# Attention edge pass: keys and values added in one instruction, one value in four added by GpSimd, one mask in four made by VectorE, and another order of the work on VectorE and ScalarE

## The chip, the cores and the metric

The kernel runs on one core of a Trainium2 chip. The time is the device time of one execution in microseconds (us), and a kernel is judged by the median of several runs. The core has five engines that run beside each other and meet only at semaphores: TensorE (PE in the rows; PEld is its weight load), VectorE (DVE), ScalarE (ACT), GpSimd (POOL) and SyncE (SP), which here only starts transfers.

## What is computed

A graph network on 6250 nodes of 256 numbers and 100000 edges, sorted by their destination. First a weighted sum over the edges with two linear layers and a normalization, then two transformer convolutions with 4 heads of 64 channels, then a last normalization. Nearly all the time that matters here goes to the two convolutions:

```
e = (edge_attr @ We).reshape(-1, H, C)
kj = k[src] + e
vj = v[src] + e
logits = jnp.einsum('ehc,ehc->eh', q[dst], kj) / np.sqrt(C)
m = jax.lax.stop_gradient(jax.ops.segment_max(logits, dst, num_segments=n))
ex = jnp.exp(logits - m[dst])
denom = jax.ops.segment_sum(ex, dst, num_segments=n)
a = ex / (denom[dst] + 1e-16)
agg = jax.ops.segment_sum(vj * a[:, :, None], dst, num_segments=n)
return agg.reshape(n, H * C) + x @ Ws + bs
```

## The kernel before

`edge_pass_attention` runs twice, as phases e1 and e2, one for each convolution. A step `i` handles one tile of 128 edges, one edge per partition, and there are T = 832 steps in a pass. Steps are counted in batches of 26 (`BATCH`, 32 batches a pass), after each of which a softmax over the batch's logits is worked off in eight small stages, two steps apart (`PACE`); and in quads of four (`QUAD`, 208 a pass), because some work is done once for four steps. Each engine has its own program, a loop over the steps, and takes its instructions strictly in that order.

What one step does, engine by engine:

- GpSimd gathers the key and value rows of the 128 source nodes from HBM into `kv`, a ring of NG = 6 tiles (line 1303, a DMA whose descriptors GpSimd makes itself). Gather `i` waits until VectorE has read the tile of step `i - 6` (`vj_done`). Once in a quad it also makes `pick` for four steps (line 1294), the one-hot matrix with which TensorE later fetches the queries.
- TensorE multiplies the edge attributes by `We` into PSUM (`e_e` in the rows, lines 1315 and 1316; each matmul stands as two instructions in the trace). In every fourth step of a quad this product isn't computed: it was made in an earlier phase, and SyncE loads it into `made`. Then TensorE fetches the queries (line 1325), and, 43 steps later, sums the weighed values by node with the matrix `mask` (line 1366).
- VectorE adds the edge's product to the keys (line 1416) and to the values (line 1420) in two instructions of 256 columns, takes four dot products of 64 columns, one for each head (line 1428), and adds an earlier step's sums to the accumulator `acc` (line 1510). The stages of the softmax stand behind that.
- ScalarE works 42 steps (LAG) behind: it makes the one-hot `mask` of step `n = i - LAG` by two activations of 128x128 (lines 1561 and 1567) and weighs the values by four activations of 65 columns, one for each head (line 1571). Its share of the softmax (lines 1543, 1546, 1551 and 1554) stands ahead of that in a step. For the last 42 steps of a pass (`LATE`), VectorE makes the mask and weighs the fourth head.

The keys and the values lie in `kvj`: two tiles for keys, and a ring of NV = 44 for values. The softmax's exponent on ScalarE (line 1546) waits for a subtraction on VectorE (line 1474). The loops for VectorE and ScalarE in the kernel before:

```
for i in range(END):
    if i < T:
        logits(i)
    if LATE <= i - LAG < T:
        late_part(i - LAG)
    if 0 <= i - LAG - 2 < T:
        add_sums(i - LAG - 2)
...
    j, step = step_at(i)
    if j is not None:
        softmax(j, step)
```

## Time and profile before

| | us |
|---|---|
| median of 3 runs | 4820.88 (4820.83 to 4821.61) |
| the profiled execution, its own time | 4832.06 |
| its span | 4830.3 |
| e1, first to last gather on GpSimd | 1365.2 to 2908.6 |
| e2, first to last gather on GpSimd | 3126.3 to 4640.0 |
| busy over the span: PE, DVE, ACT, POOL | 87%, 83%, 62%, 65% |

The profile is of one execution. Its shares are means over phases of very different kinds; the two attention passes are the two stretches in which ScalarE is busy. Durations of neighbouring instructions on VectorE, ScalarE and TensorE overlap a little in the trace, because one starts while the one before drains: what one costs its engine is the distance from start to start.

### The profile page before, as it was taken

How to read it: one execution, taken by the hardware profiler on the slowest of the kernel's cores; microseconds unless marked ns; L12 is line 12 of the kernel's file. 1: busy time of each engine (PE TensorE's matmuls, PEld its weight loads, DVE VectorE, ACT ScalarE, POOL GpSimd, SP SyncE). 2: the span in 40 equal slices, each digit the busy share in tenths (PEclk: the TensorE clock that was granted, in tenths of full speed). 3: DMA queues.
4: the chain of work that ended last, by engine and by line, in shares of the span. 5: the costliest groups of instructions: out<-in, count | busy, mean ns of one | idle time of the engine just before them, and what ended most of it. 6: DMA issues, size and time to landing. Idle time of an engine off the chain costs nothing. (4 is left out here: it accounts for less than half of the span.)

```text
span 4830.3 us, 107746 instructions
## 1 busy us (share of the span) xinstructions
PE 4189.2 (87%) x17694; PEld 3210.6 (66%) x17694; DVE 3989.0 (83%) x22772; ACT 2982.2 (62%) x10607; POOL 3116.4 (65%) x2996
## 2 busy tenths in 40 slices
PE   2887887888979999999999998889999999999988
PEld 2766666675547777777777774567777777777755
DVE  4655555556869999999999998789999999999986
ACT  1111111112319898989898984149999999989971
POOL 6677777740067777777777771287777777777730
PEclk9999999999999999999999999999999999999989
DMA  4666666654568887878788773587777777777734
GB/s 121 189 192 196 192 193 193 191 167 149 169 212 237 233 236 232 233 229 236 231 234 228 231 230 104 173 247 231 226 230 228 231 228 227 226 228 231 226 114 149
DMA packets 663064, 996.73 MB, mean 206 GB/s; under 512 B 99667, under 2 KB 489690, under 8 KB 662407
## 3 DMA queue, kind: packets, MB, share of 16 engines
q0 software_dynamic: 171408, 540.40, 38.1%
q1 hardware_dynamic: 491000, 449.44, 30.8%
q14 instruction: 471, 3.86, 0.3%
q8 instruction: 185, 3.03, 0.3%
HBM read 870.01 MB, written 119.44 MB: 205 GB/s over the span
## 5 line engine op out<-in xcount | busy, mean ns | idle before, releaser
L1303 POOL DMA_INDIRECT e_kv<-kv,src x1664 | 1635.0, 983 | 748.1 <-DVE e_kvj L1420 449.7
L1571 ACT ACTIVATE e_vals<-e_kvj,e_ex 128x65 f32<-128x65 f32 x6572 | 1725.1, 334 | 5.5 <-PE e_sum L1366 5.1
L1366 PE MATMUL e_sum<-e_vals,e_mask 128*128 128x260 f32 x3328 | 1063.7, 403 | 206.2 <-ACT e_vals L1571 190.0
L1325 PE MATMUL e_q<-q,e_pick 128*128 x3328 | 1017.2, 387 | 95.3 <-DVE e_logit L1428 66.4
L1428 DVE CUSTOM_DVE_ANT_0 e_kvj<-e_kvj,e_q 128x64 f32<-128x64 f32 x6656 | 1060.2, 214 | 3.4 <-PE e_q L1325 2.2
L152 POOL DMA_INDIRECT e_x<-x_rows,e_src x783 | 747.3, 954 | 263.1 <-issue 172.3
L1366 PEld LDWEIGHTS e_sum<-e_vals,e_mask 128*128 128x128 f32 x3328 | 563.0, 190 | 454.4 <-issue 379.7
L1325 PEld LDWEIGHTS e_q<-q,e_pick 128*128 128x128 f32 x3328 | 618.2, 191 | 252.4 <-issue 169.9
L1315 PE MATMUL e_e<-e_we,e_ea 112*128 112x256 f32 x2496 | 752.3, 382 | 17.4 <-DMA e_ea<-attr_tiles 16.2
L1316 PE MATMUL e_e<-e_we,e_ea 112*128 112x256 f32 x2496 | 745.8, 380 | 0.0
L1510 DVE TENSOR_TENSOR acc<-acc,e_sum 128x260 f32 x1664 | 697.3, 419 | 41.4 <-issue 23.6
L530 ACT ACTIVATE q<-e_edges 128x512 f32<-128x512 f32 x208 | 124.2, 597 | 925.5 <-PE e_edges L523 921.7
L1294 POOL TENSOR_SCALAR e_pick<-e_spots,own 128x512 f32<-128x512 bf16 x416 | 660.9, 1589 | 15.4 <-DMA e_spots<-locals 1.1
L1567 ACT ACTIVATE e_mask<-e_apart,one 128x128 f32<-128x128 f32 x1580 | 634.6, 402 | 52.5
L597 PE MATMUL e_sum<-e_x,e_mask 128*128 x1664 | 455.2, 400 | 210.6 <-DVE e_mask L612 114.0
L620 DVE TENSOR_TENSOR acc<-acc,e_sum 128x256 f32 x832 | 349.9, 421 | 332.0 <-PE e_sum L597 308.0
L1561 ACT ACTIVATE e_apart<-iota,local 128x128 f32<-128x128 f32 x1580 | 610.4, 386 | 0.0
L1416 DVE TENSOR_TENSOR e_kvj<-e_kv,e_e 128x256 f32<-128x256 f32 x1248 | 513.4, 411 | 66.2 <-DMA e_kv<-kv,src 40.3
L1315 PEld LDWEIGHTS e_e<-e_we,e_ea 112*128 112x128 f32 x2496 | 477.7, 192 | 96.4 <-issue 20.3
L1420 DVE TENSOR_TENSOR e_kvj<-e_kv,e_e 128x256 f32<-128x256 f32 x1248 | 514.7, 412 | 21.0 <-ACT e_vals L1571 20.6
L1428 DVE DVE_READ_ACCUMULATOR2_ANT e_logit<- 128x1 f32 x6656 | 531.6, 80 | 0.2 <-issue 0.2
L597 PEld LDWEIGHTS e_sum<-e_x,e_mask 128*128 128x128 f32 x1664 | 316.9, 198 | 312.2 <-issue 270.2
(223 smaller groups left out, 4479.1 us busy)
## 6 DMA issues: line engine op xcount, KB each, us to landing
e_ea<-attr_tiles SPq DMA_DIRECT2D x1248, 112.0 KB
edges<-q SPq DMA_DIRECT2D x208, 256.0 KB
e_spots<-locals SPq DMA_DIRECT2D x416, 128.0 KB
e_made<-edges SPq DMA_DIRECT2D x416, 128.0 KB
e_kv<-kv,src POOLq DMA_INDIRECT x1664
kv<-n_proj_rows SPq DMA_DIRECT2D x98, 256.0 KB
q<-attr_tiles SPq DMA_DIRECT2D x208, 112.0 KB
n_x<-x_rows SPq DMA_DIRECT2D x98, 128.0 KB
```

The costliest lines, as they stand in the source:

```text
L152: e.indirect_dma_start(out=self.x[:, at:at + D], out_offset=None, **rows_of(self.t["x_rows"], self.src[:, i:i + 1])).then_inc(self.got[i / ...
L597: e.matmul(sums[i % SUMS][:, 0:D], mask[:, i % R, :], rows, start=True, stop=True).then_inc(summed, 1)
L1294: e.tensor_scalar(pick[:, c % 2, :], spots[:, c % 2, :], k["own"][:, 0:1], None, ALU.is_equal).then_inc(picked, 1)
L1303: e.indirect_dma_start(out=kv[:, u, :], out_offset=None, **rows_of(kv_rows, k["src"][:, i:i + 1])).then_inc(kv_got[u], 16)
L1315: e.matmul(pe_e[a % 2][:, 0:D], ea[:, a % NE, 0:P], we[:, 0, :], start=True, stop=False)
L1316: e.matmul(pe_e[a % 2][:, 0:D], ea[:, a % NE, P:2 * P], we[:, 1, :], start=False, stop=True).then_inc(e_done, 1)
L1325: e.matmul(pe_q[i % 2][:, 0:D], pick[:, c, at:at + P], rows, start=True, stop=True).then_inc(q_done, 1)
L1366: e.matmul(sums[n % 2][:, 0:VALS], mask[:, n % R, :], vals[:, n % R, :], start=True, stop=True).then_inc(summed, 1)
L1428: dot = e.tensor_tensor_reduce(kvj[:, i % 2, h, 0:C], kvj[:, i % 2, h, 0:C], pe_q[i % 2][:, hs], 1.0, 0.0, ALU.mult, ALU.add, logit[:, j % ...
L1510: e.tensor_tensor(rows, rows, sums[n % 2][:, 0:VALS], ALU.add).then_inc(added, 1)
L1567: e.activation(mask[:, n % R, :], apart[:], ACT.Relu, bias=k["one"][:, 0:1], scale=-1.0).then_inc(masked, 1)
L1571: by_weight = e.activation(vals[:, n % R, h * HV:(h + 1) * HV], kvj[:, 2 + n % NV, h, :], ACT.Copy, scale=ex[:, b % 2, h, r:r + 1])
```

## The change

Three things change inside `edge_pass_attention`, and nothing outside it.

In three steps of four the two additions become one instruction of 512 columns that reads the edge product twice. In the fourth step of each quad VectorE adds only the keys, and GpSimd adds the values (`last_values`), between two gathers; the next gather waits for that addition, since it overwrites the tile that the addition reads, and the load of `made` waits for it too.

The mask of every fourth step, those with `n % QUAD == 0`, is made by VectorE in one comparison (`make_mask`), where ScalarE took two activations. In the late steps VectorE makes all masks, as before, now by this function.

The order changes. On VectorE, the dot products of a step move from behind its additions to behind the mask, the late part and the addition to `acc`. On ScalarE, the mask and the weighing move ahead of the softmax's part.

The core of the diff:

```diff
+        def vector_masks(n):
+            return n >= LATE or n % QUAD == 0
+
+        def vector_masks_before(n):
+            return -(-min(n, LATE) // QUAD) + max(n - LATE, 0)
+
...
                 def load_made(c):
                     if c >= 2:
-                        e.wait_ge(vj_done, (c - 1) * QUAD)
+                        e.wait_ge(kvj_done, (c - 1) * QUAD)
+                        e.wait_ge(values_done, c - 1)
...
+                def last_values(c):
+
+                    i = QUAD * c + QUAD - 1
+                    e.wait_ge(kv_got[i % NG], 16 * (i // NG + 1))
+                    e.wait_ge(made_got[c % 2], 16 * (c // 2 + 1))
+                    if i >= NV:
+                        e.wait_ge(weighed, i - NV + 1)
+                    by_head = "p (h c) -> p h c"
+                    e.tensor_tensor(kvj[:, 2 + i % NV, :, 0:C], kv[:, i % NG, D:].rearrange(by_head, h=H),
+                                    made[:, c % 2, :].rearrange(by_head, h=H), ALU.add).then_inc(values_done, 1)
+
+                def gather(i):
+                    u = i % NG
+                    if i >= NG:
+                        e.wait_ge(kvj_done, i - NG + 1)
+                        if (i - NG) % QUAD == QUAD - 1:
+                            last_values((i - NG) // QUAD)
+                            e.wait_ge(values_done, (i - NG) // QUAD + 1)
+                    e.indirect_dma_start(out=kv[:, u, :], out_offset=None,
+                                         **rows_of(kv_rows, k["src"][:, i:i + 1])).then_inc(kv_got[u], 16)
+
                 e.memset(kvj[:], 1.0).then_inc(ones_set, 1)
+                e.wait_ge(ones_set, 1)
                 for i in range(T):
-                    u = i % NG
                     if i % QUAD == 2:
                         pick_rows(i // QUAD)
-                    if i >= NG:
-                        e.wait_ge(vj_done, i - NG + 1)
-                    e.indirect_dma_start(out=kv[:, u, :], out_offset=None,
-                                         **rows_of(kv_rows, k["src"][:, i:i + 1])).then_inc(kv_got[u], 16)
-                e.wait_ge(ones_set, 1)
+                    gather(i)
+                for c in range((T - NG) // QUAD, s.quads):
+                    last_values(c)
 
...
                     if i >= 2:
                         e.wait_ge(dots_done, i - 1)
-                    e.tensor_tensor(kvj[:, i % 2, :, 0:C], kv[:, i % NG, 0:D].rearrange("p (h c) -> p h c", h=H), edge,
-                                    ALU.add).then_inc(kj_done, 1)
-                    if i >= NV:
-                        e.wait_ge(weighed, i - NV + 1)
-                    e.tensor_tensor(kvj[:, 2 + i % NV, :, 0:C], kv[:, i % NG, D:].rearrange("p (h c) -> p h c", h=H), edge,
-                                    ALU.add).then_inc(vj_done, 1)
-                    e.wait_ge(kj_done, i + 1)
+                    if at < QUAD - 1:
+                        if i >= NV:
+                            e.wait_ge(weighed, i - NV + 1)
+                        e.tensor_tensor(kvj[:, key_at:value_at + 1:value_at - key_at, :, 0:C],
+                                        kv[:, i % NG, :].rearrange("p (a h c) -> p a h c", a=2, h=H),
+                                        edge.unsqueeze(1).to_broadcast([P, 2, H, C]), ALU.add).then_inc(kvj_done, 1)
+                    else:
+                        e.tensor_tensor(kvj[:, key_at, :, 0:C], kv[:, i % NG, 0:D].rearrange("p (h c) -> p h c", h=H), edge,
+                                        ALU.add).then_inc(kvj_done, 1)
+
+                def dots(i):
+                    j, r = i // BATCH, i % BATCH + 1
+                    e.wait_ge(kvj_done, i + 1)
...
+                def make_mask(n):
+                    if n >= R:
+                        e.wait_ge(summed, n - R + 1)
+                    e.tensor_tensor(mask[:, n % R, :], k["iota"][:], k["local"][:, n:n + 1].to_broadcast([P, P]), ALU.is_equal).then_inc(vector_masked, 1)
+
...
                 for i in range(END):
                     if i < T:
-                        logits(i)
+                        add_edges(i)
+                    if 0 <= i - LAG < T and vector_masks(i - LAG):
+                        make_mask(i - LAG)
                     if LATE <= i - LAG < T:
                         late_part(i - LAG)
                     if 0 <= i - LAG - 2 < T:
                         add_sums(i - LAG - 2)
+                    if i < T:
+                        dots(i)
...
+                    n = i - LAG
+                    if 0 <= n < T:
+                        b, r = n // BATCH, n % BATCH + 1
+                        made_before = n - vector_masks_before(n)
+                        if not vector_masks(n):
+                            if made_before:
+                                e.wait_ge(masked, made_before)
+                            e.activation(apart[:], k["iota"][:], ACT.Square, bias=k["local"][:, n:n + 1],
+                                         scale=-1.0).then_inc(apart_done, 1)
+                            e.wait_ge(apart_done, made_before + 1)
+                        if n >= R:
+                            e.wait_ge(summed, n - R + 1)
+                        if not vector_masks(n):
+                            e.activation(mask[:, n % R, :], apart[:], ACT.Relu, bias=k["one"][:, 0:1],
+                                         scale=-1.0).then_inc(masked, 1)
+                        e.wait_ge(ex_done, b + 1)
+                        if n % QUAD == QUAD - 1:
+                            e.wait_ge(values_done, n // QUAD + 1)
+                        for h in range(H if n < LATE else H - 1):
+                            by_weight = e.activation(vals[:, n % R, h * HV:(h + 1) * HV], kvj[:, 2 + n % NV, h, :], ACT.Copy,
+                                                     scale=ex[:, b % 2, h, r:r + 1])
+                        by_weight.then_inc(weighed, 1)
...
```

In the rows that follow, `e_kv`, `e_kvj`, `e_made`, `e_pick`, `e_mask`, `e_vals` and `e_ex` are the tiles `kv`, `kvj` and so on of the code; the number at the front is the line of the respective kernel.

GpSimd, early in e1, where the loop reaches its steady form. Before, the four gathers of a quad follow each other between two `pick`s:

```order
L1303 DMA e_kv<-kv,src 128x512 x2
L1294 TENSOR_SCALAR e_pick<-e_spots,own 128x512
L1303 DMA e_kv<-kv,src 128x512 x4
L1294 TENSOR_SCALAR e_pick<-e_spots,own 128x512
L1303 DMA e_kv<-kv,src 128x512 x4
```

And in the changed kernel, the same place:

```order
L1301 TENSOR_SCALAR e_pick<-e_spots,own 128x512
L1321 DMA e_kv<-kv,src 128x512 x3
L1311 TENSOR_TENSOR e_kvj<-e_kv,e_made 128x4x64
L1321 DMA e_kv<-kv,src 128x512
L1301 TENSOR_SCALAR e_pick<-e_spots,own 128x512
```

The addition stands behind the third gather of a quad and ahead of the fourth; the order of gathers and `pick`s among themselves is the same.

VectorE, the middle of e1, one step of the kernel before and the start of the next (a dot product is two rows, the second of which reads out its sum; the rows left out are those of the other heads):

```order
L1416 TENSOR_TENSOR e_kvj<-e_kv,e_e 128x4x64
L1420 TENSOR_TENSOR e_kvj<-e_kv,e_e 128x4x64
L1428 ISA e_kvj,e_logit<-e_kvj,e_q 128x64
L1428 ISA e_logit 128x1
...
L1510 TENSOR_TENSOR acc<-acc,e_sum 128x260
L1416 TENSOR_TENSOR e_kvj<-e_kv,e_made 128x4x64
L1420 TENSOR_TENSOR e_kvj<-e_kv,e_made 128x4x64
```

The changed kernel, a step in which VectorE makes the mask, with a softmax stage behind it, and the next one, in which it adds only keys:

```order
L1445 TENSOR_TENSOR e_kvj<-e_kv,e_e 128x2x4x64
L1547 TENSOR_TENSOR e_mask<-iota,local 128x128
L1542 ISA
L1542 TENSOR_TENSOR acc<-acc,e_sum 128x260
L1460 ISA e_kvj,e_logit<-e_kvj,e_q 128x64
L1460 ISA e_logit 128x1
...
L1497 COPY e_ends<-e_back 128x2
L1465 SCALAR_TENSOR_TENSOR e_fw<-e_pen,e_ends,e_lr 128x128
L1468 SCALAR_TENSOR_TENSOR e_mx<-e_pen,e_ends,e_fw 128x128
L1449 TENSOR_TENSOR e_kvj<-e_kv,e_made 128x4x64
```

The dot products have moved behind the addition to `acc`; the softmax's stage still ends the step.

ScalarE around the softmax's exponent, in e1. Before:

```order
L1571 ACTIVATE e_vals<-e_kvj,e_ex 128x65 x4
L1546 ACTIVATE e_lr<-e_lr 128x128
L1561 ACTIVATE e_apart<-iota,local 128x128
L1567 ACTIVATE e_mask<-e_apart,one 128x128
L1571 ACTIVATE e_vals<-e_kvj,e_ex 128x65 x4
```

In the changed kernel, from there to the copy of the weights `e_ex`:

```order
L1598 ACTIVATE e_vals<-e_kvj,e_ex 128x65 x4
L1609 ACTIVATE e_lr<-e_lr 128x128
L1586 ACTIVATE e_apart<-iota,local 128x128
L1592 ACTIVATE e_mask<-e_apart,one 128x128
L1598 ACTIVATE e_vals<-e_kvj,e_ex 128x65 x8
L1614 ACTIVATE e_ex<-e_back 128x128
```

A row of eight weighings is a step with its mask made here and the next one, whose mask comes from VectorE. The rows read alike around the exponent; by the code, the weighing that now stands ahead of it belongs to the same step of the loop, and before it belonged to the step ahead.

## Rows read from the trace of the kernel before

**Rows 1.** The page, part 2: busy tenths in 40 slices of the span.

```profile
DVE  4655555556869999999999998789999999999986
ACT  1111111112319898989898984149999999989971
POOL 6677777740067777777777771287777777777730
```

**Rows 2.** Windows: length, busy us of PE, PEld, DVE, ACT, POOL; clock, DMA, GB/s.

```profile
1700.00:2300.00 600.00, 551.60 (x2456) 439.15 (x2456) 572.88 (x3768) 543.92 (x1985) 444.40 (x404) 1.00 0.80 233
3300.00:4000.00 700.00, 639.73 (x2829) 503.66 (x2828) 674.82 (x4451) 645.39 (x2356) 527.84 (x478) 1.00 0.78 229
```

**Rows 3.** Waits in both passes: who waited for whom, us in total, times, longest.

```profile
POOL e_kv L1303 <- DVE e_kvj L1420: 449.7, 618, 3.2
ACT e_lr L1546 <- DVE e_lr L1474: 204.8, 64, 20.4
PE e_sum L1366 <- ACT e_vals L1571: 190.0, 308, 1.7
DVE e_kvj L1416 <- DMA e_kv<-kv,src: 46.1, 30, 12.0
```

**Rows 4.** Timeline of VectorE in e1: start, us, what.

```profile
1652.05 0.42 DVE L1416 TENSOR_TENSOR e_kvj<-e_kv,e_made 128x256 f32<-128x256 f32 x1
1652.39 0.42 DVE L1420 TENSOR_TENSOR e_kvj<-e_kv,e_made 128x256 f32<-128x256 f32 x1
...
1653.62 0.41 DVE L1416 TENSOR_TENSOR e_kvj<-e_kv,e_e 128x256 f32<-128x256 f32 x1
```

**Rows 5.** Timeline of GpSimd in e1, one quad and the next pick.

```profile
1608.36 1.58 POOL L1294 TENSOR_SCALAR e_pick<-e_spots,own 128x512 f32<-128x512 bf16 x1
1610.11 1.04 POOL L1303 DMA_INDIRECT e_kv<-kv,src  x1 [0.17 <-issue]
1611.45 0.94 POOL L1303 DMA_INDIRECT e_kv<-kv,src  x1 [0.31 <-issue]
...
1613.95 0.95 POOL L1303 DMA_INDIRECT e_kv<-kv,src  x1 [0.31 <-DVE e_kvj L1420]
1614.94 1.58 POOL L1294 TENSOR_SCALAR e_pick<-e_spots,own 128x512 f32<-128x512 bf16 x1
```

**Rows 6.** Groups on GpSimd, whole span: busy us, mean ns, idle before.

```profile
L1303 POOL DMA_INDIRECT e_kv<-kv,src x1664 | 1635.0, 983 | 748.1 <-DVE e_kvj L1420 449.7 <-issue 248.6 <-PE e_q L1325 49.8
L1294 POOL TENSOR_SCALAR e_pick<-e_spots,own 128x512 f32<-128x512 bf16 x416 | 660.9, 1589 | 15.4 <-DMA e_spots<-locals 1.1
L815 POOL MEMSET acc<- 128x260 f32 x49 | 15.4, 315 | 276.0 <-DVE n_y L845 276.0
L265 POOL TENSOR_SCALAR_AFFINE_SELECT ident<-ident 128x128 f32<-128x128 f32 x1 | 0.3, 294 | 0.2 <-POOL ident L263 0.2
L1647 POOL MEMSET const-float32-0.0<- 128x1 f32 x1 | 0.1, 99 | 0.3 <-issue 0.3
```

**Rows 7.** Timeline in e1: a value addition, and the gather that waited for it.

```profile
1620.19 0.40 DVE L1420 TENSOR_TENSOR e_kvj<-e_kv,e_e 128x256 f32<-128x256 f32 x1
1620.86 0.95 POOL L1303 DMA_INDIRECT e_kv<-kv,src  x1 [0.62 <-DVE e_kvj L1420]
```

**Rows 8.** Groups on VectorE in both passes: shapes like the new instructions'.

```profile
L744 DVE TENSOR_TENSOR n_proj_rows<-n_proj,n_b_proj 128x512 f32<-128x512 f32 x49 | 33.9, 691 | 5.5 <-PE n_proj L733 5.5
L1474 DVE TENSOR_TENSOR e_lr<-e_lr,e_mx 128x128 f32<-128x128 f32 x64 | 19.2, 300 | 0.0
```

**Rows 9.** Timeline of ScalarE in e1, one step.

```profile
1658.34 0.39 ACT L1561 ACTIVATE e_apart<-iota,local 128x128 f32<-128x128 f32 x1
1659.06 1.05 ACT L1571 ACTIVATE e_vals<-e_kvj,e_ex 128x65 f32<-128x65 f32 x4
1660.02 0.39 ACT L1561 ACTIVATE e_apart<-iota,local 128x128 f32<-128x128 f32 x1
```

**Rows 10.** Timeline in e1: a scan of two SBUF tensors during the pick.

```profile
1609.03 0.42 DVE L1433 TENSOR_TENSOR_SCAN e_fw<-e_pen,e_lr 128x128 f32<-128x128 f32 x1
```

43 lines of the change are left out of this document (12 added, 31 removed).

## The prediction, made before the changed kernel ran

> **What bounds the kernel now.** I look first at where the two passes are: the slices in which ScalarE is busy [rows 1]. Between them and around them the change touches nothing. One row of windows for each pass then says who is full [rows 2]: VectorE is busy 572.88 of 600 us in e1 and 674.82 of 700 in e2, 95 and 96%; TensorE 92 and 91%, ScalarE 91 and 92%, GpSimd 74 and 75%. The waits name the same engine: GpSimd waited 449.7 us for VectorE's value addition, ScalarE 204.8 us for its subtraction, and VectorE only 46.1 us for gathered rows, in 30 of 1664 steps [rows 3]. So VectorE's order of work sets the pace, and GpSimd follows it.
>
> The pace: from the first to the last gather of a pass lie 831 gathers, 207.75 quads. The passes' gathers span 1365.2 to 2908.6 and 3126.3 to 4640.0 us (the table on the time before), together 3057.1 us in 415.5 quads, **7.36 us a quad**. All sums below are a quad's length times 415.5.
>
> GpSimd's 75% hides something. A gather lasts 0.95 to 1.04 us, but the next never starts sooner than 0.30 us after it, even where it waited for nothing ("issue") [rows 5]. From pick to pick, with nothing late, that quad took 1614.94 - 1608.36 = 6.58 us. By the means of all 1664 gathers [rows 6] it is 4 x 0.983 + 1.589 + gaps of 0.02 to 0.03 ahead of the pick, 0.17 behind it and 3 x 0.30: **6.62 us**. GpSimd's real room is 7.36 - 6.62 = 0.74 us a quad, and the change puts an addition there.
>
> **VectorE, part by part.** From start to start an addition of 256 columns costs 0.34 us [rows 4], though it shows as 0.42. The 512-column addition is nearest to that of line 744, also from PSUM and SBUF, 691 ns [rows 8]: 0.27 us more than one of 0.42, so 0.61 against 2 x 0.34. Three of them save 3 x 0.07 = 0.20. The fourth step loses an addition, 0.34. The mask adds a two-input instruction of 128 columns, 300 ns in [rows 8] and about 0.22 from start to start, by the same 0.08 of overlap. Together -0.20 - 0.34 + 0.22 = -0.32: VectorE would need 7.36 - 0.32 = **7.04 us**. If it stayed the bound, the gain would be 0.32 x 415.5 = 133 us. The bounds of these three are narrow: the wide addition can't be dearer than the two it replaces (0.68, then the gain is 0.12 a quad).
>
> **ScalarE** loses two activations in every fourth step. They cost 1659.06 - 1658.34 = 0.72 us of a step of 1.68 [rows 9]; a quad falls from 6.72 to 6.00, plus the softmax's few. It wasn't the bound and gets farther from it. TensorE does what it did: 92% of 7.36 is 6.8 us a quad, under VectorE's new 7.04.
>
> **The new order.** The weighing ahead of the softmax part gives TensorE its values before ScalarE waits for the subtraction. Of TensorE's 190.0 us of waiting for weighings [rows 3], 0.46 us a quad, some goes. The dots behind the addition to `acc` now stand behind a wait for TensorE's sum, and the next queries behind the dots: that could bring some of it back. The lag between their key addition and the dots is covered by the 0.34 of `acc`, as before by the value addition. I cost both at nothing, because of the next point: GpSimd leaves VectorE 0.25 us a quad over. Without that cover they are worth at most those 0.46 us, either way.
>
> **GpSimd.** The gap of 0.30 between the third and the fourth gather becomes 0.03 (as ahead of the pick), the addition V, and a wait of the gather for V's semaphore. The row nearest to this wait is a gather held by VectorE: the value addition ended at 1620.19 + 0.40 = 1620.59, the gather began at 1620.86, 0.27 us later [rows 7]. 0.03 + 0.27 is the 0.30 that went, so a quad takes **6.62 + V**. The two queue behind: the fourth gather, the pick for the next queries, and through them VectorE's keys and TensorE's queries. V's own waits (its rows, `made`, the freed slot) were met by then in the kernel before. The load of `made` that SyncE now holds until V is done is released ahead of the gather of an earlier step than the one it serves, so it isn't later than the gathers.
>
> V itself stands nowhere in this trace. From below: a memset of 260 columns, with no input, 315 ns. From above: the whole pick, 512 columns, 1589 ns [rows 6]. Scaled to 256 columns, with the 99 ns of a one-column instruction taken as fixed: the select of 128 columns gives (294 - 99) x 2 + 99 = 489 ns, the pick (1589 - 99) / 2 + 99 = 844 ns. V has two inputs and one plain operation, between a simple one-input instruction and a comparison that also converts; I take the middle, 0.67 us. Then a quad is **7.29 us** on GpSimd against 7.04 on VectorE: the bound moves to GpSimd, and of the 0.32 only 0.07 is left. 0.07 x 415.5 = 29 us. Against that, GpSimd will now and then still wait for VectorE where a softmax stage or a block of the skip product falls, some 0.02 a quad or 8 us. The profiled execution: 4832 - 21 = 4811 us; the median lies 11 us under the profiled execution, so **4800 us**.
>
> The Trainium skill speaks against such a change: "GPSIMD Engine Reference", section "Performance versus the Vector engine", holds two-input elementwise work on GpSimd to be about half as fast as on VectorE, with 4497 ns for 2048 columns of fp32. By that page V would be an estimated (4497 - 99) / 8 + 99 = 649 ns and the sum 9 us lower; no row here shows it.
>
> **The rivals.** *VectorE stays the bound* (0.17). If V is under 0.42 us, GpSimd's quad is under 7.04. For it: the memset's 315 ns; against it, both scaled rows with an input are above. Time: 4821 - 133 = 4688 us, up to 4730 with V at 0.5.
>
> *GpSimd's addition costs more than its room* (0.30). The break-even is V = 0.74. At the pick's rate, 0.844, a quad is 7.46 us and the time 4821 + 0.10 x 415.5 + 8 = 4871 us; at the whole pick's 1589 ns, 8.21 us a quad and 5174 us, which half the columns make unlikely. For it: the pick is the one wide GpSimd operation in the pass, and three times as dear per column as the memset.
>
> *VectorE and GpSimd shut each other out* (0.05). A new two-input addition on GpSimd and VectorE's mask (two SBUF inputs) meet in every quad; if VectorE then waited V out, its quad would be 7.04 + 0.67 = 7.71 us, 4821 + 145 = 4966 us. Against it: a scan of two SBUF tensors began at 1609.03 in the middle of the pick of 1608.36 to 1609.94, and took 0.42 us [rows 5, 10]. The rule is the Trainium skill's, "SBUF — State Buffer", section "SBUF: two separate sides": a VectorE instruction with two SBUF inputs and a GpSimd instruction that reads SBUF exclude each other for their whole length. By that rule the scan should have waited; the trace doesn't agree.
>
> *My forecast, GpSimd the bound with V from 0.5 to 0.76* (0.48): 4730 to 4838 us.
>
> **How the numbers follow.** A measurement of this kernel tells about 0.2%, 10 us. Faster: the first rival 0.17, and 0.36 of my forecast's 0.48 (V under 0.70): 0.53. The same: the remaining 0.12. Slower: 0.30 + 0.05 = 0.35. The range reaches from V = 0.49 (6.62 + 0.49 = 7.11, 4821 - 104 + 8 = 4725) to V = 0.844 (4871); about 0.1 lies outside on either side.
>
> **What would show it.** GpSimd's windows: its addition at 0.6 to 0.75 us, no gap but issue gaps and the 0.27 behind the addition, a quad of about 7.3 in both passes alike, though before e1 took 7.43 and e2 7.29; so e1 gains and e2 hardly. VectorE waits for `e_kv` in hundreds of steps, not 30, and its busy share falls under 95%. The 512-column addition shows near 690 ns. ScalarE's wait for the subtraction shrinks or moves. The prediction is wrong if GpSimd still waits for VectorE for hundreds of us in total (then V or the wait behind it is cheaper), or if V is over 0.74.

## The result

The changed kernel took **4863.37 us** (median of 4 runs, 4861.23 to 4867.09) against 4820.85 before (4820.75 to 4821.61): ratio **1.0087**, 95% interval 1.0072 to 1.0103, slower by 42.5 us. The time lies inside the forecast range, on the other side of no change: the rival "GpSimd's addition costs more than its room" is what happened.

Line numbers are now those of the changed kernel: gather L1321, GpSimd's value addition L1311, pick L1301, wide addition L1445, key addition L1449, dots L1460, VectorE's mask L1547, `acc` L1542, the weighing L1598. First the page of the changed kernel, part 2, the row that answers to GpSimd's in [rows 1] and the two beside it:

```profile
DVE  4655555567869999999999998689999999999986
ACT  1111111112317888888788873057878887878770
POOL 6677777740078888888888880388888888888840
```

GpSimd went from 7 to 8 tenths in both passes, ScalarE from 8 and 9 down to 7 and 8. The windows of the changed kernel, as in [rows 2] (length, busy us of PE, PEld, DVE, ACT, POOL; clock, DMA, GB/s):

```profile
1700.00:2300.00 600.00, 554.20 (x2440) 439.38 (x2439) 562.17 (x3504) 485.31 (x1810) 505.85 (x480) 0.99 0.78 232
3300.00:4000.00 700.00, 630.82 (x2777) 497.45 (x2776) 652.94 (x4098) 571.31 (x2132) 589.22 (x561) 1.00 0.74 224
```

VectorE, 95 and 96% full before, is 94 and 93% full. GpSimd at 84% is nearly as full as this loop can make it: most of the rest is the gaps that follow its gathers and the addition. The granted clock is that of before within 0.01. The same view over exactly the two passes, first gather to last, before and then changed, only the row of sums:

```profile
sum 3057.10, PE 2773.41 PEld 2187.75 DVE 2895.09 ACT 2646.05 POOL 2293.96; mean PE 1386.70 PEld 1093.87 DVE 1447.55 ACT 1323.03 POOL 1146.98
sum 3110.70, PE 2799.40 PEld 2207.98 DVE 2870.25 ACT 2386.45 POOL 2623.86; mean PE 1399.70 PEld 1103.99 DVE 1435.13 ACT 1193.22 POOL 1311.93
```

VectorE's busy time fell by 25 us, 0.06 us a quad, where the forecast took 0.32 a quad off it. GpSimd's groups in both passes of the changed kernel, as in [rows 6] (busy us, mean ns of one, idle before):

```profile
L1321 POOL DMA_INDIRECT e_kv<-kv,src x1664 | 1640.1, 986 | 460.8 <-issue 249.2 <-POOL e_kvj L1311 95.2 <-DVE e_kvj L1445 54.8
L1301 POOL TENSOR_SCALAR e_pick<-e_spots,own 128x512 f32<-128x512 bf16 x416 | 673.2, 1618 | 17.2
L1311 POOL TENSOR_TENSOR e_kvj<-e_kv,e_made 128x256 f32<-128x256 f32 x416 | 315.2, 758 | 14.9 <-DMA e_kv<-kv,src 2.9 <-ACT e_vals L1598 2.6
```

The new addition takes 758 ns, where the forecast had 670 and the break-even 740. The first idle figure holds the other half of the story: before, gathers waited 449.7 us for VectorE [rows 3]; now 54.8 for its wide additions and 16.8 for its key additions. One quad on GpSimd, changed kernel, to be laid beside [rows 5] (start, us, what, idle before it):

```profile
1607.20 1.64 POOL L1301 TENSOR_SCALAR e_pick<-e_spots,own 128x512 f32<-128x512 bf16 x1
1609.01 1.03 POOL L1321 DMA_INDIRECT e_kv<-kv,src  x1 [0.17 <-issue]
1610.35 0.94 POOL L1321 DMA_INDIRECT e_kv<-kv,src  x1 [0.31 <-DVE e_kvj L1445]
1611.59 0.95 POOL L1321 DMA_INDIRECT e_kv<-kv,src  x1 [0.30 <-issue]
1612.56 0.75 POOL L1311 TENSOR_TENSOR e_kvj<-e_kv,e_made 128x256 f32<-128x256 f32 x1
1613.58 0.96 POOL L1321 DMA_INDIRECT e_kv<-kv,src  x1 [0.28 <-POOL e_kvj L1311]
1614.57 1.65 POOL L1301 TENSOR_SCALAR e_pick<-e_spots,own 128x512 f32<-128x512 bf16 x1
```

The gaps are those forecast: 0.02 ahead of the addition, 0.28 behind it, and one put down to VectorE at 0.31 is as long as one put down to nothing, so it isn't a wait for VectorE. This quad took 1614.57 - 1607.20 = 7.37 us. The length of the passes (first and last gather start in each, of the changed kernel):

```profile
L1321 POOL DMA_INDIRECT e_kv<-kv,src x832: 940/957/1714, 1360.5 to 2915.0; - x167
L1321 POOL DMA_INDIRECT e_kv<-kv,src x832: 940/957/1637, 3124.7 to 4680.7; - x167
```

1554.5 and 1556.0 us over 207.75 quads each are 7.483 and 7.490, **7.486 us a quad** where it was 7.358 (7.43 and 7.29): e1 and e2 are now alike, as a serial chain on one engine makes them. The passes grew by 53.4 us; the stretch between them shrank by 8.0 (3126.3 - 2908.6 before, 3124.7 - 2915.0 now), and the stretch behind e2 by 8.7 (190.3 before, 4862.3 - 4680.7 now). What VectorE and TensorE wait for now, changed kernel, both passes:

```profile
PE e_q L1351 <- DVE e_logit L1460: 168.6, 231, 2.3
PE e_q L1351 <- POOL e_pick L1301: 137.4, 139, 8.2
DVE e_kvj L1445 <- DMA e_kv<-kv,src: 103.6, 117, 12.0
ACT e_lr L1609 <- DVE e_lr L1506: 331.1, 63, 23.1
PE e_sum L1392 <- ACT e_vals L1598: 0.2, 1, 0.2
```

VectorE's wide addition waits for gathered rows in 117 steps, where 30 waited before, and TensorE waits for the pick: both are late because GpSimd is. ScalarE's wait for the subtraction grew from 204.8 us to 331.1; the prediction had it shrink or move. The last row answers to TensorE's 190.0 us in [rows 3]: that wait has gone altogether, and nothing came of it here.

### The profile page after: what moved, and what is told of

Read it like the earlier page. It is cut to its first block and busy times, and to the rows that moved or that the text cites. A ratio compares the mean times of both kernels' runs of the same rounds, so it can differ in the third digit from the quotient of the medians.

```text
span 4862.3 us, 108916 instructions
## 1 busy us (share of the span) xinstructions
PE 4198.4 (86%) x17694; PEld 3218.9 (66%) x17694; DVE 3956.2 (81%) x21504; ACT 2709.7 (56%) x9815; POOL 3446.0 (71%) x3412
## 5 line engine op out<-in xcount | busy, mean ns | idle before, releaser
L1321 POOL DMA_INDIRECT e_kv<-kv,src x1664 | 1640.1, 986 | 460.8 <-issue 249.2
L1598 ACT ACTIVATE e_vals<-e_kvj,e_ex 128x65 f32<-128x65 f32 x6572 | 1691.5, 334 | 25.4 <-PE e_sum L1392 25.2
L1351 PE MATMUL e_q<-q,e_pick 128*128 x3328 | 1059.5, 400 | 315.9 <-DVE e_logit L1460 168.6
L1460 DVE CUSTOM_DVE_ANT_0 e_kvj<-e_kvj,e_q 128x64 f32<-128x64 f32 x6656 | 1060.9, 213 | 10.8 <-PE e_q L1351 6.8
L1392 PE MATMUL e_sum<-e_vals,e_mask 128*128 128x260 f32 x3328 | 1028.5, 391 | 9.7 <-DVE acc L1542 4.9
L1351 PEld LDWEIGHTS e_q<-q,e_pick 128*128 128x128 f32 x3328 | 584.9, 192 | 605.8 <-issue 536.7
L1445 DVE TENSOR_TENSOR e_kvj<-e_kv,e_e 128x512 f32<-128x512 f32 x1248 | 846.4, 678 | 118.7 <-DMA e_kv<-kv,src 103.6
L1542 DVE TENSOR_TENSOR acc<-acc,e_sum 128x260 f32 x1664 | 692.8, 416 | 61.3 <-PE e_sum L1392 47.5
L1301 POOL TENSOR_SCALAR e_pick<-e_spots,own 128x512 f32<-128x512 bf16 x416 | 673.2, 1618 | 17.2
L1392 PEld LDWEIGHTS e_sum<-e_vals,e_mask 128*128 128x128 f32 x3328 | 594.7, 190 | 128.5 <-issue 43.5
L1341 PEld LDWEIGHTS e_e<-e_we,e_ea 112*128 112x128 f32 x2496 | 483.4, 194 | 90.6 <-issue 15.7
L1592 ACT ACTIVATE e_mask<-e_apart,one 128x128 f32<-128x128 f32 x1184 | 475.4, 402 | 105.4 <-PE e_sum L1392 65.7
L1460 DVE DVE_READ_ACCUMULATOR2_ANT e_logit<- 128x1 f32 x6656 | 527.7, 79 | 0.1
L1342 PEld LDWEIGHTS e_e<-e_we,e_ea 112*128 112x128 f32 x2496 | 477.2, 191 | 71.2
L1586 ACT ACTIVATE e_apart<-iota,local 128x128 f32<-128x128 f32 x1184 | 457.3, 386 | 0.0
```

The costliest lines, as they stand in the source:

```text
L1301: e.tensor_scalar(pick[:, c % 2, :], spots[:, c % 2, :], k["own"][:, 0:1], None, ALU.is_equal).then_inc(picked, 1)
L1321: e.indirect_dma_start(out=kv[:, u, :], out_offset=None, **rows_of(kv_rows, k["src"][:, i:i + 1])).then_inc(kv_got[u], 16)
L1341: e.matmul(pe_e[a % 2][:, 0:D], ea[:, a % NE, 0:P], we[:, 0, :], start=True, stop=False)
L1342: e.matmul(pe_e[a % 2][:, 0:D], ea[:, a % NE, P:2 * P], we[:, 1, :], start=False, stop=True).then_inc(e_done, 1)
L1351: e.matmul(pe_q[i % 2][:, 0:D], pick[:, c, at:at + P], rows, start=True, stop=True).then_inc(q_done, 1)
L1392: e.matmul(sums[n % 2][:, 0:VALS], mask[:, n % R, :], vals[:, n % R, :], start=True, stop=True).then_inc(summed, 1)
```

## The experiments

The kernels below ran on five chips, each beside the kernel before. On the first and the fourth chip the kernel before took about 5123 us, on the others 4826 to 4831. Much of that difference lies ahead of the passes: the first gather of the kernel with the new order alone came at 1573.5 us on the first chip and at 1366.3 on the third. Each ratio is against the kernel before on its own chip, with a 95% interval, and times in us are compared only within a chip. "Quad" is the time between the first and the last gather of both passes over 415.5, as above. The 7.358 of the kernel before is from its one trace; it has none on these five chips, so a difference to it is only as good as two like chips are alike (the changed kernel has 7.486 above and 7.491 on the second chip). Diffs are against the changed kernel unless the text says before.

**Which part costs?** First chip (before 5123.87 us). The first kernel leaves all additions to VectorE and all early masks to ScalarE, and keeps the wide addition (now in every step) and the new order:

```diff
-            return n >= LATE or n % QUAD == 0
+            return n >= LATE
...
-                        if (i - NG) % QUAD == QUAD - 1:
-                            last_values((i - NG) // QUAD)
-                            e.wait_ge(values_done, (i - NG) // QUAD + 1)
...
-                    if at < QUAD - 1:
+                    if True:
```

> The changed kernel without the addition on GpSimd and without the masks on VectorE: all four steps of a quad have the wide addition on VectorE, ScalarE makes the masks, the new order stays. Theory A (GpSimd's quad of 7.49 us is what set the pace of the changed kernel): GpSimd falls back to 6.6 us a quad, VectorE is the bound again with 7.36 - 4 x 0.07 = 7.09 us, and the time is 4821 - 112 = about 4710 us (4690 to 4735). Theory B (the new order, with the dots behind the wait for TensorE's sum, is what cost the time): it is still in, so the kernel stays above 4780 us.

Measured: 5047.67 us, ratio 0.9847 (0.9819 to 0.9876), quad 7.411. The times expected were for a chip like that of the result; as ratios, theory A had 0.977 and theory B at least 0.991, and the kernel came out between them. The second kernel gives up only VectorE's masks (the first two lines of that diff, and the count of masks that goes with them):

> The changed kernel with every mask made by ScalarE again, as before the change; the addition on GpSimd stays. Theory A: GpSimd stays the bound; only what VectorE's mask does to the pick (1.618 us on average against 1.589) goes, 0.03 us a quad or 12 us: 4850 us (4835 to 4865). Theory C (VectorE's mask and GpSimd shut each other out, and VectorE lost the time there): without the masks the kernel falls by over 40 us, under 4825.

Measured: 5058.88 us, 0.9872 (0.9843 to 0.9902), quad 7.454. The third makes GpSimd's addition twice, its result as before:

```diff
+                    e.tensor_tensor(kvj[:, 2 + i % NV, :, 0:C], kv[:, i % NG, D:].rearrange(by_head, h=H),
+                                    made[:, c % 2, :].rearrange(by_head, h=H), ALU.add).then_inc(values_once, 1)
+                    e.wait_ge(values_once, c + 1)
                     e.tensor_tensor(kvj[:, 2 + i % NV, :, 0:C], kv[:, i % NG, D:].rearrange(by_head, h=H),
                                     made[:, c % 2, :].rearrange(by_head, h=H), ALU.add).then_inc(values_done, 1)
```

> The changed kernel with the GpSimd addition made twice in a row, the second waiting for the first; the result is the same. Theory A: all of it lands on the time, 0.74 us and a wait of about 0.2 between the two, 0.94 x 415.5 = 390 us: 5255 us (5220 to 5290). If GpSimd had slack left (theories B, C), a part of it would hide, and the time would rise by under 300 us.

Measured: 5422.27 us, 1.057 (1.0541 to 1.0599), quad 8.333, 0.85 over the 7.486 of the changed kernel (0.94 expected). Its GpSimd, one quad:

```profile
1810.82 0.96 POOL L1325 DMA_INDIRECT e_kv<-kv,src  x1 [0.30 <-issue]
1811.80 0.74 POOL L1312 TENSOR_TENSOR e_kvj<-e_kv,e_made 128x256 f32<-128x256 f32 x1
1812.62 0.73 POOL L1315 TENSOR_TENSOR e_kvj<-e_kv,e_made 128x256 f32<-128x256 f32 x1
1813.62 0.96 POOL L1325 DMA_INDIRECT e_kv<-kv,src  x1 [0.28 <-POOL e_kvj L1315]
1814.62 1.71 POOL L1302 TENSOR_SCALAR e_pick<-e_spots,own 128x512 f32<-128x512 bf16 x1
```

From start to start the extra one costs 0.82 here, and the quad grew by all of it: nothing hides any part of GpSimd's addition. The fourth is the kernel before with the new order alone:

```diff
-                def logits(i):
-                    j, r = i // BATCH, i % BATCH + 1
+                def add_edges(i):
...
+                def dots(i):
+                    j, r = i // BATCH, i % BATCH + 1
...
-                        logits(i)
+                        add_edges(i)
...
                         add_sums(i - LAG - 2)
+                    if i < T:
+                        dots(i)
```

and on ScalarE the block `j, step = step_at(i) ...` moved behind the weighing.

> The kernel before with only the new order: the dots behind the addition to acc on VectorE, the softmax's part behind the weighing on ScalarE; two additions of 256 columns, all masks on ScalarE, nothing new on GpSimd. Theory A: no loss; TensorE waits less for weighings, 4821 us less 0 to 60: 4790 us. Theory B: slower than 4821 us by 20 us or more.

Measured: 5049.71 us, 0.9842 (0.9815 to 0.9869), quad 7.421. The term costed at nothing gains by itself. What stayed unclear was that the kernel with GpSimd's addition and no masks on VectorE gained too on this chip, where the changed kernel wasn't measured.

**On a chip like that of the result.** Second chip (before 4831.48). The changed kernel itself:

> The changed kernel once more, unaltered, beside the kernel before on whatever chip this is. The four kernels ahead of it ran on a chip where the kernel before took 5124 us. Theory A (GpSimd sets the pace of the changed kernel): its quads take 7.49 us on any chip, since GpSimd waits there for nothing but itself; where the kernel before takes 4821 us it is 0.9% slower, where it takes 5124 us it is 1% or more faster. If instead the two kernels lose the same time on the slower chip, the ratio is 1.008 there too.

Measured: 4868.69 us, 1.009 (1.0067 to 1.0114), quad 7.491: the result again. The wide addition in the order of before, without GpSimd's addition and VectorE's masks:

> The kernel before with one thing alone: the two additions of every step as one of 512 columns; old order, all masks on ScalarE, nothing new on GpSimd. The dots now stand right behind the addition whose end they wait for. Theory A: four additions save 4 x 0.07 us a quad, the dots' wait for the addition costs 0.1 to 0.2 us a step, 4 x 0.15: 0.3 us a quad slower than the kernel before, +2.5% (0 to +4%). Rival: the wait is short (under 0.07 us), and the kernel is up to 2% faster.

Measured: 4894.24 us, 1.0128 (1.0111 to 1.0145), quad 7.520. In the old order the wide addition loses. Its groups on VectorE in both passes, without the last steps of e2, say why:

```profile
L1454 DVE CUSTOM_DVE_ANT_0 e_kvj<-e_kvj,e_q 128x64 f32<-128x64 f32 x6492 | 1048.2, 218 | 59.9 <-PE e_q L1345 3.9 <-issue 0.3
L1439 DVE TENSOR_TENSOR e_kvj<-e_kv,e_e 128x512 f32<-128x512 f32 x1218 | 826.1, 678 | 102.9 <-ACT e_vals L1604 55.7 <-DMA e_kv<-kv,src 36.6 <-PE e_e L1336 5.8
```

The dots stood idle 59.9 us where it was 3.4: they need the end of the addition right ahead of them, which the value addition had covered. Nor can they start while it drains: from its start to theirs it costs 0.68 us on the mean, against 0.62 in the changed kernel. And the keys now wait for ScalarE too (55.7 us), since one instruction also needs the freed slot for the values. GpSimd's addition on the order of before, with two narrow additions on one semaphore, which the dots wait for:

> The kernel before with one thing alone: GpSimd adds the values of every fourth step; two additions of 256 columns in the others, old order, all masks on ScalarE. Theory A: GpSimd is the bound as in the changed kernel, 7.45 us a quad, a little less than the changed kernel's 7.49 as no mask disturbs the pick: 0.8% slower than before on the chip of 4821 us. Rival (the loss needs the new order or the mask too): same as before or faster, since VectorE saves 0.34 us a quad.

Measured: 4927.35 us, 1.0202 (1.0185 to 1.0219), quad 7.612. Its dots wait for the second narrow addition, so it mixes two causes; a run further down takes them apart. GpSimd's addition in every second quad only:

```diff
+        def by_pool(i):
+            return i % (2 * QUAD) == 2 * QUAD - 1
...
-                        if (i - NG) % QUAD == QUAD - 1:
+                        if by_pool(i - NG):
...
-                    if at < QUAD - 1:
+                    if not by_pool(i):
```

> The changed kernel with GpSimd's addition in every second quad only, the wide addition on VectorE in the others. Theory A: GpSimd's quad falls by half of 0.76 + 0.03 to 7.1 us, VectorE's rises by 0.14 to about 7.2 to 7.3 us, and the two share the bound: 7.25 us a quad, 0.24 less than the changed kernel or 2% faster than it, and 1 to 1.5% faster than before on the chip of 4821 us. Rival (VectorE, the order or the mask is what cost the time): no faster than the changed kernel.

Measured: 4729.49 us, **0.9795** (0.9778 to 0.9813), quad 7.155. Its windows:

```profile
1700.00:2300.00 600.00, 568.76 (x2546) 453.83 (x2544) 582.62 (x3664) 507.08 (x1893) 502.74 (x459) 1.00 0.82 242
3300.00:4000.00 700.00, 651.61 (x2882) 514.32 (x2882) 676.77 (x4255) 590.95 (x2205) 586.22 (x539) 1.00 0.78 234
```

VectorE is back at 97%, and GpSimd is as full as in the changed kernel. Half of the work moved costs far less than all of it; whether it gains anything over none is for the next chip.

**What each part is worth on one chip.** Third chip (before 4826.06). The new order alone again, the wide addition with it, then with GpSimd's addition added, and half of GpSimd's without VectorE's masks:

> The kernel before with only the new order, once more, hoped to be on a chip where the kernel before takes near 4821 us. If the order by itself gains (the addition of all parts without it took 7.61 us a quad, the changed kernel 7.49): 1 to 2% faster than before. If the first run's 1.6% was the slow chip's alone: within 0.5% of before.

Measured: 4702.16 us, **0.9745** (0.9729 to 0.9762), quad 7.071.

> New order and four wide additions on VectorE, all masks on ScalarE, nothing on GpSimd, once more. Theory A: with GpSimd out of the way, VectorE needs 0.28 us a quad less than before, and the stalls between engines fall too: 2 to 3.5% faster than before, near 7.1 us a quad. Rival (TensorE or ScalarE holds the quad at 7.3 and more): under 1.5% faster.

Measured: 4670.99 us, **0.9674** (0.9658 to 0.969), quad 7.002, the fastest kernel of the study.

> The changed kernel with all masks on ScalarE, once more. Theory A: GpSimd's quad decides again, 7.45 us as on the other chip: 0.4 to 0.8% slower than before where before takes 4821 us. Theory C: without VectorE's masks it is faster than before.

Measured: 4854.75 us, 1.0056 (1.004 to 1.0073), quad 7.459.

> GpSimd's addition in every second quad, and all masks on ScalarE. GpSimd has 7.1 us a quad, VectorE 0.2 us less than with the masks, 7.0. If VectorE was the bound of the half version at 7.155 us a quad: 7.1, 0.5 to 1% faster than it, 2.5 to 3% faster than before. If ScalarE, with 6.7 us a quad of its own and the softmax, needs the room that the mask gave it: slower than the half version.

Measured: 4719.19 us, 0.9784 (0.9768 to 0.9801), quad 7.113. So here the order gains 124 us, the wide addition 31 more, and GpSimd's addition, which takes an addition of 256 columns off VectorE, costs 184. In every second quad it still costs 48 (4719.19 - 4670.99), and that kernel is slower than the order alone: with this order, no share of the work that was tried gains on GpSimd. With the masks back on ScalarE the half version's ratio is 0.9784, against 0.9795 with them on VectorE: no difference beyond the intervals. Waits of the kernel with order and wide addition:

```profile
POOL e_kv L1317 <- DVE e_kvj L1439: 285.7, 547, 2.5
PE e_q L1345 <- DVE e_logit L1454: 109.4, 183, 2.1
```

and its windows:

```profile
1700.00:2300.00 600.00, 578.05 (x2584) 461.10 (x2583) 578.22 (x3633) 569.25 (x2086) 468.75 (x424) 1.00 0.83 246
3300.00:4000.00 700.00, 669.96 (x2983) 530.27 (x2981) 682.96 (x4303) 676.86 (x2480) 553.91 (x503) 1.00 0.81 241
```

VectorE is 96 and 98% busy, TensorE 96 and 96, ScalarE 95 and 97: three engines close together, GpSimd at 78 and 79% and waiting for VectorE.

**Which half of the order?** Fourth chip (before 5123.27). Two kernels have narrow additions, nothing new on GpSimd and no masks on VectorE: the first has the new order on ScalarE alone, with VectorE's dots right behind its additions, the second has it on VectorE alone. The third is the changed kernel without GpSimd's addition.

> The kernel before with only ScalarE's half of the new order: mask and weighing ahead of the softmax's part; VectorE keeps its order. Theory D (TensorE waited 190 us for weighings that stood behind ScalarE's wait for the subtraction, and that wait spread to VectorE): most of the 2.6% is here, 1.5 to 2.6% faster than before, and TensorE's wait for weighings falls to some 20 us. Theory E (the dots' place gives the gain): within 0.5% of before.

Measured: 5158.16 us, 1.0068 (1.0045 to 1.009), quad 7.666. Theory D's gain didn't come: it is slower. Its dots wait for the end of the second narrow addition, a stall that the kernel before hasn't (81.0 us of idle time ahead of them, against 3.4), so it says nothing clean on ScalarE's half. But TensorE's wait for weighings is gone in it too: to take that wait away isn't enough by itself.

> The kernel before with only VectorE's half of the new order: the dots behind the addition to acc; ScalarE keeps its order. Theory D: within 0.7% of before, and TensorE still waits near 190 us for weighings. Theory E: 1.5% or more faster than before.

Measured: 5190.99 us, 1.0131 (1.0109 to 1.0152), quad 7.729. VectorE's half alone loses.

> The changed kernel with the fourth step's values added on VectorE by the wide addition: order, wide additions and VectorE's masks stay, nothing new on GpSimd. Against the version without VectorE's masks (3.3% faster than before): a mask costs VectorE 0.22 us a quad and what the pick holds it up. Theory A (VectorE is the bound there): 0.2 to 0.3 us a quad or 80 to 120 us slower than that version, 0.8 to 1.6% faster than before. Rival (ScalarE or TensorE is the bound there): as fast as that version or faster.

Measured: 5025.11 us, 0.9804 (0.9776 to 0.9832), quad 7.373: with VectorE's masks kept and GpSimd's addition gone, it is faster than before, and by its ratio no slower than the kernel without masks on the like first chip (0.9847). The rival holds: there VectorE isn't the bound, and its masks cost nothing that shows.

**The same, cleanly.** Fifth chip (before 4827.49). The kernel before with ScalarE's block moved and nothing else:

```diff
-                    j, step = step_at(i)
-                    if step == 0:
...
                     n = i - LAG
                     if 0 <= n < T:
...
+                    j, step = step_at(i)
+                    if step == 0:
...
```

> The kernel before with one edit: ScalarE weighs a step's values ahead of its softmax part (scale, exponentials), as in the change. VectorE's order, additions and masks, and GpSimd, are those of before. Theory D (ScalarE's half relieves TensorE): TensorE's 190 us of waiting for weighings go, VectorE's order stays, and the quad falls from 7.36 towards 7.07, the quad of both halves together; the time falls by 1 to 2.6%. Theory E (the halves gain only together, since VectorE's dots right behind its additions are late for TensorE's queries or for ScalarE's subtraction either way): within 0.5% of before.

Measured: 4683.22 us, **0.9701** (0.9685 to 0.9718), quad 7.028. TensorE's waits in both passes, the first row from the kernel before, the others from this one, beside [rows 3]:

```profile
PE e_q L1325 <- DVE e_logit L1428: 66.4, 106, 2.4
PE e_q L1325 <- DVE e_logit L1428: 116.9, 231, 2.2
PE e_sum L1366 <- ACT e_vals L1554: 19.3, 58, 1.0
```

Its windows, beside [rows 2], and its sums over exactly the two passes:

```profile
1700.00:2300.00 600.00, 576.22 (x2571) 458.55 (x2570) 590.90 (x3953) 566.15 (x2075) 465.14 (x422) 1.00 0.83 244
3300.00:4000.00 700.00, 668.76 (x2960) 524.89 (x2959) 694.56 (x4672) 672.27 (x2464) 551.51 (x500) 1.00 0.81 239
sum 2920.30, PE 2760.69 PEld 2177.79 DVE 2848.59 ACT 2636.85 POOL 2294.28; mean PE 1380.34 PEld 1088.89 DVE 1424.30 ACT 1318.42 POOL 1147.14
```

The weighings no longer hold TensorE: 190.0 us became 19.3, though 50 of that came back as a longer wait for VectorE's dots. The quad fell by 7.358 - 7.028 = 0.33 us, 137 us in all. VectorE's share of that can be read: it stood idle 3057.10 - 2895.09 = 162 us in the passes before and 2920.30 - 2848.59 = 72 now, and its busy time fell by 47. Two of its groups before:

```profile
L1510 DVE TENSOR_TENSOR acc<-acc,e_sum 128x260 f32 x1664 | 697.3, 419 | 41.4 <-issue 23.6 <-PE e_sum L1366 12.1
L1420 DVE TENSOR_TENSOR e_kvj<-e_kv,e_e 128x256 f32<-128x256 f32 x1248 | 514.7, 412 | 21.0 <-ACT e_vals L1571 20.6
```

Now the first is idle for 8.6 us and the second for 0.0: TensorE's sums and the value slots that ScalarE frees both come in time. VectorE's half alone:

> The kernel before with the other edit alone: VectorE's dots stand behind the addition to acc, ScalarE as before. On another chip, beside its own kernel before, this was 1.3% slower. Theory D: ScalarE's half carries the gain, VectorE's half alone costs 0.5 to 1.5% here too. Theory E: also slower, since either half alone does nothing or harms; what tells the theories apart is the other kernel of this call. If VectorE's half alone gains here, both fall, and the loss belonged to the other chip's late rows.

Measured: 4869.16 us, 1.0083 (1.0065 to 1.0102), quad 7.448; its TensorE still waits 159.1 us for weighings. Last, the kernel before with GpSimd's addition alone, the dots waiting for the key addition only:

```diff
-                        e.wait_ge(vj_done, i - NG + 1)
+                        if (i - NG) % QUAD == QUAD - 1:
+                            e.wait_ge(kj_done, i - NG + 1)
+                            last_values((i - NG) // QUAD)
+                            e.wait_ge(values_done, (i - NG) // QUAD + 1)
+                        else:
+                            e.wait_ge(vj_done, vector_values(i - NG + 1))
```

> The kernel before with one edit: GpSimd adds the values of every fourth step, and VectorE's dots wait for the key addition alone, so that no narrow second addition stands in their way. Theory A (GpSimd's serial chain of four gathers, pick and addition is the bound): the quad is that of the changed kernel and of the one without VectorE masks, 7.45 to 7.50, and the time 0.5 to 1.0% over before. Theory B (in the old order the two engines also wait for each other): the quad is 7.55 to 7.65 and the time 1.5 to 2.2% over before, with GpSimd waiting for VectorE for over 50 us.

Measured: 4874.83 us, 1.0095 (1.0077 to 1.0112), quad 7.478. Its groups on GpSimd, both passes:

```profile
L1324 POOL DMA_INDIRECT e_kv<-kv,src x1664 | 1637.9, 984 | 465.7 <-issue 280.9 <-POOL e_kvj L1308 91.9 <-DVE e_kvj L1443 45.6
L1308 POOL TENSOR_TENSOR e_kvj<-e_kv,e_made 128x256 f32<-128x256 f32 x416 | 311.9, 750 | 26.5 <-ACT e_vals L1598 11.0 <-DVE e_kvj L1438 5.7
```

Old order or new, wide or narrow, masks or not: with GpSimd's addition the quad is 7.459 to 7.491, and 7.454 for the kernel without masks on the chip where before takes 5124 us. The 7.612 of the mixed kernel came with its dots' wait, and went with it.

## Why the prediction was wrong

**What bounds the kernel before: right in part.** VectorE was the fullest engine, but its queue order wasn't the whole of it: with no instruction taken from it, ScalarE's new order raised its windows from 95 and 96% to 98 and 99% (590.90 of 600 us, 694.56 of 700) and gained 3.0%. VectorE's 4 to 5% of idle time and TensorE's wait for weighings, which the reading took for slack, went with 137 us of the passes.

**The term that failed: V, the time of GpSimd's addition, and with it a chain held at its best.** The forecast took V as 0.67 us, the middle of 0.489 and 0.844. Measured: 0.737 at the median, and 0.758 on the mean, which is what a quad pays: over the break-even of 0.74. V lies at three quarters of the way from 0.489 to 0.844, nearer to the pick's rate. The sum made again with the measured parts: 4 x 0.986 + 1.618 + 0.758 = 6.32, idle (460.8 + 17.2 + 14.9) / 416 = 1.18, together 7.50 against 7.486 by the starts (the idle sum holds waits at the edges of the stages). Of the 0.196 that 7.486 lies over the forecast 7.29, V is 0.088, the pick 0.029, the gathers 4 x 0.003 = 0.012, and the remaining 0.067 idle time, of which 0.02 was allowed for the softmax stages. So V alone takes the forecast gain away: with 6.62 + 0.758 = 7.38 the kernel would be about level with before. Most of the 53 us that the passes grew by is the other 0.108 a quad, 45 us: the 6.62 was a chain in which nothing is late and no instruction is slowed. The sign hung on the 0.07 us between 0.67 and 0.74, with bounds 0.35 apart, and a chance of 0.53 for faster was more than such a middle carries.

**VectorE's parts: each near, their sum wrong.** The wide addition takes 678 ns on the mean (forecast near 690), the mask 0.28 us alone (forecast 0.30) and 0.38 on the mean of 452. But VectorE's busy time fell by 0.06 us a quad, not by 0.32. Taken from each start to the next over both passes, the additions save 0.46 a quad (forecast 0.54), the masks cost 0.30 (forecast 0.22, from the undisturbed length), and the softmax's stages, with the rescaling of `acc`, cost 0.14 more than before, which the sum had at nothing: GpSimd's addition gets in their way, which is the rival on shut-out engines in a small measure. On the third chip, where the kernels with and without that addition differ in nothing else (7.459 and 7.002), the same stages took 47 us more with it. The loss stayed out of the time because GpSimd was the bound. Without GpSimd's addition the wide one gained 0.07 a quad (7.071 to 7.002), not 4 x 0.07: by then TensorE and ScalarE are as full as VectorE.

**"The new order: I cost both at nothing."** For the change as a whole that held, for the reason given: GpSimd was the bound and swallowed it. The bound "at most 0.46 us, either way" was set by the right row, and the true value was seven tenths of it: ScalarE's half alone is worth 0.33 us a quad, VectorE's half alone costs 0.09, both together are worth 0.29 (on another chip). It was the largest effect in the change, and a forecast that had given it would have named the order as what to keep. What went with it was TensorE's wait for weighings, 190.0 to 19.3 us; in VectorE's half alone it stayed at 159.1. Of VectorE's 90 us less idle time, 33 stood ahead of `acc` and 21 ahead of the value additions. No run changes one of these releases alone, so which of them carries the gain stays open.

**The ends of the passes weren't in the sum.** The order shortened the stretches between and behind the passes by 16.7 us (in the kernel with ScalarE's half alone, 14.0; with GpSimd's addition in the old order they grew by 2.6). With the first gather 4.7 us earlier, the spans differ by 53.4 - 16.7 - 4.7 = 32.0 us. The profiled execution before was 11.2 us over its median, that of the changed kernel only 0.7 (4864.09 against 4863.37), so the medians differ by 32.0 + 11.2 - 0.7 = 42.5.

**The engines in each other's way: the rival was waved off too soon.** It was given 0.05 on one scan that ran during a pick [rows 10]. That scan began 0.67 us into the pick. The same trace, of the kernel before, has others (start, us, what; scans and GpSimd's rows only):

```profile
2384.06 1.59 POOL L1294 TENSOR_SCALAR e_pick<-e_spots,own 128x512 f32<-128x512 bf16 x1
2384.30 0.75 DVE L1433 TENSOR_TENSOR_SCAN e_fw<-e_pen,e_lr 128x128 f32<-128x128 f32 x1
```

The 11 scans of two SBUF tensors that began in the first 0.6 us of a pick took 0.67 us on the mean, the 66 that began later in one 0.45, and the 175 that met no pick 0.46. In the changed kernel, beside GpSimd's two-input addition:

```profile
1627.43 0.73 POOL L1311 TENSOR_TENSOR e_kvj<-e_kv,e_made 128x256 f32<-128x256 f32 x1
1627.59 0.86 DVE L1465 TENSOR_TENSOR_SCAN e_fw<-e_pen,e_ends,e_lr 128x128 f32<-128x128 f32 x1
1628.44 0.96 POOL L1321 DMA_INDIRECT e_kv<-kv,src  x1 [0.28 <-POOL e_kvj L1311]
1628.49 0.48 DVE L1468 TENSOR_TENSOR_SCAN e_mx<-e_pen,e_ends,e_fw 128x128 f32<-128x128 f32 x1
```

Two scans of one size: the one that overlaps the addition takes 0.86 us, the next 0.48. Of the 128 scans of L1465, the 26 that overlap such an addition take 0.83 on the mean, the 58 that meet neither an addition nor a pick 0.447. The Trainium skill, "SBUF — State Buffer", section "SBUF: two separate sides", has a VectorE instruction with two SBUF inputs and a GpSimd one that reads SBUF exclude each other for the whole instruction; beside the addition the trace agrees, beside the pick it agrees only around the pick's start. VectorE's mask shows the same: 0.28 us where it meets neither, 0.46 on the mean of the 90 that began in the first 0.6 us of a pick, 0.28 for the 124 that began later in one, but 0.56 for the 102 that began in the 0.7 us ahead of one, as here (changed kernel):

```profile
1614.09 0.69 DVE L1547 TENSOR_TENSOR e_mask<-iota,local 128x128 f32<-128x128 f32 x1
```

The pick that begins at 1614.57 takes 1.65 us, against 1.58 at the median. The price in time is small, though: with masks back on ScalarE the pick is 1597 ns and the quad 7.459, with them on VectorE 1617 and 7.491, so the masks cost 0.03 a quad, 13 us (two like chips). The rival's form "VectorE waits V out in every quad", 4966 us, didn't come: the dots (213 ns, 214 before) and the addition to `acc` (416, 419 before), which read PSUM too, weren't longer.

The Trainium skill's "GPSIMD Engine Reference", section "Performance versus the Vector engine", spoke against the change, rightly: 0.73 us here against VectorE's 0.34. The estimate of 649 ns worked out from its figure was 0.09 us under the median of 0.737, so the sum by it had the wrong sign too.

## What to carry to other kernels

When work moves to an engine that looks three quarters busy, add up its serial chain with the gaps that its own issue leaves, and compare that with the period: here "75% busy" was 90% of the period, and the 0.07 us that the new instruction was to leave of the room was smaller than the 0.35 between its bounds. Such a chain read where nothing is late is a floor, not a forecast: the new work also slows what stands beside it. Where a change bundles an order with a shift of work, price the order on its own, with the waits that it removes on the other full engines as the bound; here ScalarE's weighing ahead of its softmax part is worth 3.0% by itself, and with VectorE's dots behind `acc` and the wide addition 3.3% (4670.99 us), while the shift of work to GpSimd gives all of it back.

## What the runs showed of the hardware

The addition on GpSimd and the mask on VectorE in the changed kernel, each operation's own line (min/median/max ns, first and last start):

```profile
L1311 POOL TENSOR_TENSOR e_kvj<-e_kv,e_made x416: 723/737/995, 1374.7 to 4685.4; 128x256 f32<-128x256 f32 x139
L1547 DVE TENSOR_TENSOR e_mask<-iota,local x480: 252/285/879, 1442.6 to 4721.3; 128x128 f32<-128x128 f32 x160
```

- GpSimd's addition of 128x256 fp32 from SBUF to SBUF takes 0.737 us at the median, where VectorE's takes 0.34 from start to start; beside a two-input VectorE instruction (the rescaling of `acc`, at 4088 us) it went up to 0.995.
- A VectorE scan of two SBUF tensors, 0.447 us alone, takes 0.83 when it overlaps that addition. Beside GpSimd's pick of 1.6 us, scans are slowed when they begin in its first 0.6 us (0.67, kernel before) or shortly ahead of it (four, 0.72 to 0.99), and not when they begin later in it (0.45).
- One VectorE addition of 512 columns takes 0.68 us, and 0.62 from its start to the next instruction's where that one needn't wait for its end; two of 256 take 2 x 0.34.
- The kernel with GpSimd's addition and no masks on VectorE, bound by GpSimd, keeps its quad between the two kinds of chip (7.454 and 7.459); others don't (order alone 7.421 and 7.071, wide with order 7.411 and 7.002). That is why GpSimd's addition seems cheap on one chip (0.9872 against 0.9842 for the order alone) and costs 3 to 4% on another: on the chip at 5124 us something else had already stretched the quad to where GpSimd is. What stretches it wasn't tried and stays open; GpSimd's own instructions aren't it (the mean gather of the order alone takes 976 ns there and 980 on the other chip).
